# Flamingo layer with a mixture of experts on one core: keys of the first batch ahead, last V sum and last expert rows moved up, constant matmuls in the routing

## The chip, the cores and the metric

The kernel is written for Trainium2 and runs on one core. The metric is the device time of the kernel in microseconds (us), the median over runs. Five engines work side by side, each through its own list in order, and wait for each other through counters (semaphores): TensorE (PE, matmuls into PSUM), VectorE (DVE), ScalarE (ACT), GpSimd (POOL), SyncE (SP, which here only starts transfers). ACT, SP and POOL each start DMA transfers from their own queue.

## The reference, cut to what matters

Four batches of 512 tokens with 256 features (16 tiles of 128 tokens, "T"), a context of 1,601 rows per batch, and 8 experts of which each token uses 2.

```python
x = x + tanh(g_xattn) * xattn(layernorm(x), ctx, seg_id, Wq, Wkv, Wo)
x = x + tanh(g_ffn) * ffn(layernorm(x), gate_w, w1, b1, w2, b2)

def xattn(q, kv_src, seg_id, Wq, Wkv, Wo):      # 16 heads of 16
    qh = heads(q @ Wq.T); k, v = split(kv_src @ Wkv.T)
    # each token looks at 4 context rows: seg_id, seg_id-1, -2, -3
    scores = (qh . k_sel) * 16**-0.5; probs = softmax(masked scores over the 4)
    return (probs . v_sel) @ Wo.T

def ffn(x, gate_w, w1, b1, w2, b2):
    top_v, top_i = top_k(softmax(x @ gate_w.T), 2)
    # out = sum over the two experts e: top_v[e] * (silu(x @ w1[e] + b1[e]) @ w2[e] + b2[e])
```

## The kernel before

**Start.** SP loads the segment numbers, Wkv, Wq, Wo and x of batches 1 to 3 (L366 to L371), ACT the first 128 context rows of all batches (`ctx0`, one transfer), x of batch 0 and small things (L594 to L602). TensorE turns Wkv (L825) and the context (L831) by transposes. ScalarE and VectorE copy them out of PSUM; `keys_values(b)` (L857) makes keys and values of a batch, which go through `kv_sb` to a table `near_rows` in HBM, one per batch (L397). If no segment number is 128 or above, the rows beyond 128 aren't needed; that is the case here, and the branches under `general` are not taken. GpSimd's `gather(u)` (L514) fetches for the 128 tokens of tile u their 4 rows of keys and values (1 MB) by an indirect DMA; it runs 4 tiles ahead and has 8 slots. `first_norms` computes 1/sigma and the shift of the layer norm on GpSimd, first for batch 0, then after gather(0) for the other twelve tiles at once.

**Attention, 16 steps t.** VectorE's `step(t)`: product of the keys with the query (L1207), sum by head (L1211), mask, maximum, exponent on ScalarE (L644), sum, reciprocal, `prob` (L1232); within it `residual(t-2)` (L1241, L1244) and `second_moments(t-2)` (L1250). After step 0 VectorE also makes `gate2` (L1256) and `b2_lo` (L1258). GpSimd multiplies V by `prob` (`values`, L489; for the last tile it does half of the columns and VectorE the other half, L1264), makes the second norm (`norms`, L496 to L504) and the low half of each token (`remainder`, L526). TensorE: `query` (L874), `first_turn` (L882), `values` (L893: sums the 4 rows and turns them), `outputs` (L902, Wo), `second_turn` (L915), `logits` (L926). ScalarE: `first_x` (L631), `first_turned` (L638), `attended` (L652, copy of what `values` made), `second_x` (L661), `first_half` (L668), `token_out` (L673), `second_turned` (L679), `logits_kept` (L684). The order on each engine is written out by hand; after the loop comes a tail in which the last tiles are interleaved. SP loads the experts' weights (16 transfers of 1 MB, L362) during the steps and stores each x (L414).

**Routing.** VectorE runs a chain of small operations in which each waits for the one before through the counter `rt` (`link`): softmax and top 2 for tiles 0 to 11 while the last four tiles are still in work, then for these, cumulated counts, the list of tiles by expert, `order_i`, the tile count `tiles_i` (`RT_TILES`), the slots' rows `slot_row` (`RT_SLOT`), `tile_e` (`RT_LIST`). TensorE helps with short matmuls (L976 to L1006 and the list, L990), ScalarE with `pad_hot`, `e_col`, `e_pad` (L762 to L772).

**Experts.** Tiles of 128 slots, at least 32 (`FULL`) and here 37. Step q (`expert_steps`): TensorE makes the up product of tile q+1 (`up_chunk`, L1034, 48 matmuls of 128 columns) and the down product of tile q-1 (`down_chunk`, L1048 to L1056), interleaved while q+1 < FULL and one behind the other after that, and turns tile q+2 (L1062). ScalarE applies SiLU (L798) and splits weights (L780). VectorE copies the turned tile (L1449), splits weights (L1426), splits h in two 16-bit halves (`halves`, L1438 and L1440) and scales the finished rows (L1469, L1472). GpSimd gathers tokens (L576) and adds the rows to the output (L584), each addition only after the one before has landed.

## Time and profile before

| what | us |
|---|---|
| median of 3 runs (lowest, highest) | 364.44 (364.33, 365.71) |
| profiled execution | 364.77 |
| its span in the trace | 363.1 |
| busy: TensorE matmuls | 308.9 (85%) |
| busy: VectorE | 270.9 (75%) |
| busy: GpSimd | 204.8 (56%) |
| busy: ScalarE | 172.6 (48%) |

The busy shares are means over stages with different limits. In the stretch 45 to 60 us VectorE is busy for 14.24 of 15 us, in 150 to 200 us TensorE for 50.00 of 50, and between 110 and 130 TensorE for only 5.83 of 20. The profiled execution is 1.7 us longer than its span.

### The profile page before, as it was taken

The page shows a single profiled execution, that of the slowest core. Times are in us where ns is not written, and L with a number is a line of the kernel's source. Part 1 is how long each engine was busy: PE and PEld are TensorE (multiplying, and loading weights), DVE is VectorE, ACT ScalarE, POOL GpSimd, SP SyncE. Part 2 cuts the span into 40 slices and gives each one's busy share as a digit, 9 for nine tenths or more (in the row PEclk, how much of TensorE's full clock was granted, in tenths as well). Part 3 has the DMA queues.
Part 4 walks back from the last instruction along what each step waited for, and adds up shares of the span by engine and source line. Part 5 has one row for each costly group of instructions (what it writes and reads, how often), then busy time and mean ns, then how long its engine had stood idle before and what let it go on. Part 6 is the DMA issues. An engine that isn't in the chain of part 4 may idle for free.

```text
span 363.1 us, 10808 instructions
## 1 busy us (share of the span) xinstructions
PE 308.9 (85%) x3168; PEld 252.7 (70%) x3168; DVE 270.9 (75%) x641; ACT 172.6 (48%) x486; POOL 204.8 (56%) x226
## 2 busy tenths in 40 slices
PE   2767989999973349999999999999999999998910
PEld 2436878889862248788888888888888888786600
DVE  4848999999948976868878788787887776566510
ACT  1422256565454447655565565655656544324200
POOL 2286588886763052465737757477574675452330
PEclk9996999999995559999999999999999999999975
DMA  7689999999999421132323233233232332322121
GB/s 229 211 293 391 412 409 405 409 367 361 308 382 387 145 61 34 17 50 49 54 46 60 38 58 48 46 61 47 46 50 45 61 50 42 62 31 31 20 31 14
DMA packets 31388, 53.20 MB, mean 147 GB/s; under 512 B 4818, under 2 KB 25538, under 8 KB 29284
## 3 DMA queue, kind: packets, MB, share of 16 engines
q0 software_dynamic: 9408, 26.63, 28.8%
q1 hardware_dynamic: 16100, 22.57, 17.4%
q10 hardware_dynamic: 5824, 3.26, 3.0%
q8 instruction: 33, 0.54, 0.6%
q14 instruction: 23, 0.19, 0.2%
HBM read 42.29 MB, written 10.17 MB: 144 GB/s over the span
## 4 chain that ended last, share of the span: by engine, by line
PE 66%; POOL 10%; DVE 8%; issue 6%; DMA 6%; ACT 2%; POOLq 0%; SPq 0%; ACTq 0%; DVEq 0%
PE ps L1034 27%; PE ps L1048 15%; PE ps L1051 8%; PE ps L893 3%; DMA sel<-near_rows,win_near 3%; PE ps L1062 2%; PE ps L1056 2%; POOL w_parts L489 2%; POOL sel L489 2%; PE ps L902 2%; DMA w_parts<-in_L_xattn_Wkv 2%; POOL sel L514 1%; PE ps L1055 1%; PE ps L1050 1%; POOL rstd L499 1%
## 5 line engine op out<-in xcount | busy, mean ns | idle before, releaser
L1034 PE MATMUL ps<-sel,w_parts 128*128 128x128 f16 x1776 | 142.3, 221 | 0.6 <-DVE sel L1449 0.6
L1034 PEld LDWEIGHTS ps<-sel,w_parts 128*128 x1776 | 120.7, 99 | 25.0 <-issue 1.1
L798 ACT ACTIVATE sel<-ps,b1T 128x128 f32<-128x128 f32 x296 | 84.5, 369 | 92.4 <-PE ps L1034 86.8
L584 POOL DMA_INDIRECT out<-sel x37 | 62.7, 1694 | 88.7 <-DVE sel L1472 79.4
L1048 PE MATMUL ps<-w_parts,sel 128*128 x259 | 96.3, 379 | 2.1 <-DVE sel L1440 1.9
L1051 PE MATMUL ps<-w_parts,sel 128*128 x259 | 70.6, 273 | 0.0
L1440 DVE SCALAR_TENSOR_TENSOR sel<-sel 128x512 f16<-128x512 f32 x74 | 51.3, 693 | 2.5
L576 POOL DMA_INDIRECT sel<-tokens_split,sel x37 | 42.0, 1136 | 19.4 <-DVE sel L1408 12.7
L1426 DVE SCALAR_TENSOR_TENSOR w_parts<-w_parts (+1 forms) x32 | 39.0, 1220 | 8.6 <-issue 6.4
L571 POOL TENSOR_TENSOR sel<-sel 128x1 f32<-128x1 f32 x37 | 40.3, 1090 | 3.4 <-PE ps L1062 3.4
L1438 DVE TENSOR_SCALAR sel<-sel 128x512 f16<-128x512 f32 x74 | 33.1, 447 | 8.9 <-ACT sel L798 8.6
L780 ACT ACTIVATE w_parts<-w_parts (+1 forms) x32 | 34.1, 1067 | 7.9 <-issue 4.3
L1449 DVE COPY sel<-ps 128x512 f16<-128x512 f16 x37 | 15.7, 424 | 29.0 <-PE ps L1062 20.7
L1048 PEld LDWEIGHTS ps<-w_parts,sel 128*128 128x128 f16 x259 | 25.3, 98 | 7.6 <-issue 2.9
L1051 PEld LDWEIGHTS ps<-w_parts,sel 128*128 128x128 f16 x259 | 25.3, 98 | 3.7
L902 PE MATMUL ps<-WT,aT 128*128 128x256 f32 x64 | 18.4, 409 | 2.6 <-ACT aT L652 1.8
L874 PE MATMUL ps<-WT,xnT 128*128 128x256 f32 x64 | 17.1, 391 | 4.0 <-ACT xnT L638 4.0
L1469 DVE TENSOR_SCALAR xn<-ps,sel 128x256 f32<-128x256 f32 x37 | 17.7, 479 | 3.7 <-PE ps L1056 3.1
L893 PEld LDWEIGHTS ps<-ident,sel 128*128 128x128 f32 x128 | 16.9, 209 | 3.5 <-POOL sel L489 3.2
L489 POOL TENSOR_TENSOR sel<-sel,prob 128x1024 f32<-128x1024 f32 x8 | 15.6, 1952 | 6.3 <-DVE prob L1232 6.3
L893 PE MATMUL ps<-ident,sel 128*128 128x128 f32 x128 | 17.6, 296 | 1.7 <-POOL sel L489 1.7
L1062 PE MATMUL ps<-ident,sel 128*128 128x128 f16 x148 | 14.8, 224 | 4.9 <-DMA sel<-tokens_split,sel 4.9
(220 smaller groups left out, 441.4 us busy)
## 6 DMA issues: line engine op xcount, KB each, us to landing
w_parts<-in_L_ffn_w SPq DMA_DIRECT2D x16, 1024.0 KB
out<-xs SPq DMA_DIRECT2D x16, 128.0 KB
tokens_split<-xsplit ACTq DMA_DIRECT2D x16, 128.0 KB, 6.2
xs<-in_x SPq DMA_DIRECT2D x3, 512.0 KB, 11.0
near_rows<-w_parts SPq DMA_DIRECT2D x4, 256.0 KB, 2.9
sel<-tokens_split,sel POOLq DMA_INDIRECT x37, 2.9
out<-sel POOLq DMA_INDIRECT x37
w_parts<-in_ctx ACTq DMA_DIRECT2D x1, 512.0 KB, 4.3
```

What stands on the lines that cost most here:

```text
L571: pool.tensor_tensor(slot_w[:, at(q + 1)], xg[(k + 1) % 4][:, bass.ds(e + D, 1)], valid[:, at(q + 1)], ALU.mult).then_inc(s["slot_w_ok"], 1)
L576: pool.indirect_dma_start(xg[k], None, xd, bass.IndirectOffsetOnAxis(slot_row[:, at(q + 4)], 0))\
L584: pool.indirect_dma_start(out_rows, bass.IndirectOffsetOnAxis(slot_row[:, at(q - 1)], 0), y_sb[(k + 3) % 4], None, compute_op=ALU.add).the ...
L780: act.activation(part(to, 0), place(raw), ACT.Copy, scale=W_SCALE).then_inc(s["w_hi_ok"], 1)
L798: act.activation(h32[n][:, c * P:c * P + P], ps_h[n][:, c * P:c * P + P], ACT.Silu, bias=biases[:, c:c + 1], scale=1.0 / (X_SCALE * W_SCALE))\
L893: mm = pe.matmul(ps_a[:, c * P:c * P + P], slot(u)[:, j, D + c * P:D + c * P + P], ident[:, :], start=(j == 0), stop=(j == WIN - 1))
L1034: mm = pe.matmul(ps_h[n][:, c * P:c * P + P], w, xx, start=(i == 0), stop=(i == len(products) - 1))
L1048: pe.matmul(sides, hi, both, start=(c == 0), stop=False)
L1051: mm = pe.matmul(ps_y[n][:, 0:D], lo, rhi, start=False, stop=False)
L1426: v.scalar_tensor_tensor(out=part(to, 1), in0=place(raw), scalar=W_SCALE, in1=part(to, 0), op0=ALU.mult, op1=ALU.subtract).then_inc(s["w_l ...
L1438: v.tensor_scalar(h_hi[n][:, cols], h32[n][:, cols], H_SCALE, None, ALU.mult).then_inc(s["hhi_ok"], 1)
L1440: v.scalar_tensor_tensor(out=h_lo[n][:, cols], in0=h32[n][:, cols], scalar=H_SCALE, in1=h_hi[n][:, cols], op0=ALU.mult, op1=ALU.subtract). ...
```

## The change

It does seven things.
1. The context of batch 0 is loaded and turned by itself (`ctx_in0`, `context_turn`), ahead of Wkv; `keys_values(0)` follows directly. The other contexts come on SP's queue and are turned after query(0). x of batches 2 and 3 is loaded after the write of batch 0's keys.
2. Gather(1) goes ahead of the second `first_norms`; VectorE and ScalarE get the copies of the keys in another order.
3. `b2_lo` moves from VectorE to GpSimd, `gate2` behind the attention; the shift of the second norm is one operation per column on GpSimd instead of two in a chain.
4. In the tail of the attention, `values(T - 1)` comes before second_turn(T-4), its second column half first; `attended(T - 1)` and `logits_kept` change places on ScalarE.
5. TensorE gets 51 matmuls of 256 columns on constants, whose result nobody reads (`spin`).
6. `r_end` and `tiles_i` are computed after the slots.
7. For the tiles from FULL on, VectorE scales the finished rows (`rows_out`) before the first halves of the next tile.

```diff
 # SP
-            for b in range(1, B):
+            sp.dma_start(ctx0[:, 1:B, :], ctx_first[:, 1:B, :]).then_inc(s["ctx_in1"], 16)
+
+            def tokens_in(b):
                 sp.dma_start(xs[:, TPB * b:TPB * b + TPB, :], x_v[:, TPB * b:TPB * b + TPB, :]).then_inc(s[f"x_in{b}"], 16)
+            tokens_in(1)
...
             for b in range(B):
-                sp.wait_ge(s[f"kv_ok{b // 2}"], b % 2 + 1)
+                if b == 2:
+                    sp.wait_ge(s["kv_ok1"], 1)
+                else:
+                    sp.wait_ge(s["kv_ok0"], min(b, 2) + 1)
                 sp.dma_start(kv_near[b], kv_sb[:, b, :]).then_inc(s[f"kv_out{b}"], 16)
+                if b == 0:
+                    tokens_in(2)
+                    tokens_in(3)
 # GpSimd
-                pool.tensor_tensor(shift2[:, some], mv2[:, some, 0], rstd2[:, some], ALU.mult)\
-                    .then_inc(s["shift2_ok"], 1)
-                pool.wait_ge(s["shift2_ok"], 2 * i + 1)
-                pool.tensor_scalar(shift2[:, some], shift2[:, some], -1.0, None, ALU.mult)\
-                    .then_inc(s["shift2_ok"], 1)
+                for c in range(some.start, some.stop):
+                    last = pool.tensor_scalar(shift2[:, c:c + 1], mv2[:, c:c + 1, 0], rstd2[:, c:c + 1], -1.0, ALU.mult,
+                                              ALU.mult)
+                last.then_inc(s["shift2_ok"], 1)
...
-            gather(0)
+            for u in range(2):
+                gather(u)
             first_norms(2, slice(TPB, T))
-            for u in range(1, 4):
+            for u in range(2, 4):
                 gather(u)
+            pool.wait_ge(s["b2_hi_ok"], 1)
+            pool.tensor_scalar(b2_raw[:, :], b2_raw[:, :], 16.0, None, ALU.mult).then_inc(s["b2_lo_ok"], 1)
+            pool.wait_ge(s["b2_lo_ok"], 1)
+            pool.tensor_tensor(b2_lo[:, :], b2_raw[:, :], b2_hi[:, :], ALU.subtract).then_inc(s["b2_lo_ok"], 1)
 # ScalarE
-            act.dma_start(ctx0, ctx_first).then_inc(s["ctx_in"], 16)
+            act.dma_start(ctx0[:, 0, :], ctx_first[:, 0, :]).then_inc(s["ctx_in0"], 16)
...
             first_x(0)
+            act.wait_ge(s["wT_ps"], 1)
+            act.activation(WqT.rearrange("p k c -> p (k c)"), ps[:, 6, :], ACT.Copy).then_inc(s["wT_ok"], 1)
+            act.wait_ge(s["segt_ps"], 1)
+            first_turned(0)
             first_x(1)
-            first_turned(0)
+            act.activation(WoT.rearrange("p k c -> p (k c)"), ps[:, 7, :], ACT.Copy).then_inc(s["wT_ok"], 1)
             act.wait_ge(s["kv_ps"], 2)
             act.activation(kv_sb[:, 1, :], kv_bank[1], ACT.Copy).then_inc(s["kv_ok0"], 1)
             first_x(2)
             first_turned(1)
+            act.wait_ge(s["kv_ps"], 4)
+            act.activation(kv_sb[:, 3, :], kv_bank[3], ACT.Copy).then_inc(s["kv_ok0"], 1)
...
             first_half(T - 4)
+            token_out(T - 5)
+            attended(T - 1)
             logits_kept(T - 5)
             second_turned(T - 4)
-            token_out(T - 5)
-            logits_kept(T - 4)
             second_x(T - 3)
-            attended(T - 1)
             first_half(T - 3)
             token_out(T - 4)
             act.wait_ge(s["rt"], RT_SHIFT)
             act.activation(r_ex[:, 0:LATE, :], r_tmp[:, 0:LATE, :], ACT.Exp).then_inc(s["rt_exp"], 1)
+            logits_kept(T - 4)
             second_x(T - 2)
 # TensorE
+            pe.wait_ge(s["ctx_in0"], 16)
+            context_turn(0, 0, 0).then_inc(s["ctxT_ps"], 1)
             pe.wait_ge(s["wkv_in"], 16)
...
+            keys_values(0)
...
+            first_turn(0)
+            query(0)
+            pe.wait_ge(s["ctx_in1"], 16)
+            context_turn(1, 3, 0)
+            context_turn(2, 3, 256).then_inc(s["ctxT_ps"], 1)
+            context_turn(3, 2, 0).then_inc(s["ctxT_ps"], 1)
+            keys_values(1)
+            first_turn(1)
             pe.wait_ge(s["wT_ok"], 2)
-            pe.wait_ge(s["ctxT_ok1"], 1)
-            first_turn(0)
-            keys_values(1)
-            query(0)
-            first_turn(1)
             for b in range(2, B):
                 keys_values(b)
...
             outputs(T - 2)
+            values(T - 1)
             second_turn(T - 4)
             logits(T - 5)
-            values(T - 1)
+            outputs(T - 1)
             logits(T - 4)
-            outputs(T - 1)
             pe.matmul(ps_base, ones16[:, :], r_cum[:, :, :].rearrange("p e t -> p t e"), start=False, stop=True)\
                 .then_inc(s["rt_ps"], 1)
+
+            def spin(n):
+                for _ in range(n):
+                    pe.matmul(ps[:, 5, 0:2 * P], ones16[:, :], twice[:, :, :], start=True, stop=True)
+
+            spin(16)
             pe.wait_ge(s["rt"], RT_FIRST)
...
+            spin(4)
             pe.wait_ge(s["pad_hot_ok"], E + 1)
             for e in range(E):
                 mm = pe.matmul(ps_pad[0:E, 0:P], tok_e[:, e, :], pad_hot[:, e, :], start=(e == 0), stop=(e == E - 1))
             mm.then_inc(s["pad_ps"], 1)
+            spin(4)
             pe.wait_ge(s["rt"], RT_ROWS)
             rows_into_list(0, 8)
+            spin(2)
...
             rows_into_list(16, 24)
+            spin(1)
             pe.wait_ge(s["rt"], RT_ROWS + 3)
             rows_into_list(24, 2 * T).then_inc(s["list_ps"], 1)
+            spin(24)
 # VectorE
             first_norm(0)
-            for b in range(1, B):
-                first_norm(b)
-            for b in range(2, B):
-                dve.wait_ge(s["kv_ps"], b + 1)
-                v.tensor_copy(kv_sb[:, b, :], kv_bank[b]).then_inc(s["kv_ok1"], 1)
+            first_norm(1)
+            dve.wait_ge(s["ctxT_ps"], 2)
+            v.tensor_copy(ctxT[:, 1:3, :, :].rearrange("p b k c -> p (b k c)"), ps[:, 3, :]).then_inc(s["ctxT_ok1"], 1)
+            dve.wait_ge(s["ctxT_ps"], 3)
+            v.tensor_copy(ctxT[:, 3, :, :].rearrange("p k c -> p (k c)"), ps[:, 2, 0:256]).then_inc(s["ctxT_ok1"], 1)
+            first_norm(2)
+            first_norm(3)
+            dve.wait_ge(s["kv_ps"], 3)
+            v.tensor_copy(kv_sb[:, 2, :], kv_bank[2]).then_inc(s["kv_ok1"], 1)
...
-            link(v.tensor_tensor(r_end[:, :], r_first[:, :], r_tf[:, :], ALU.add))
-            link(v.tensor_reduce(tiles_i[:, :], r_end[:, :], AX_X, ALU.max))
-            assert done[0] == RT_TILES
...
             assert done[0] == RT_SLOT
+            link(v.tensor_tensor(r_end[:, :], r_first[:, :], r_tf[:, :], ALU.add))
+            link(v.tensor_reduce(tiles_i[:, :], r_end[:, :], AX_X, ALU.max))
...
+                if q + 1 >= FULL and live(-1):
+                    rows_out(q, k, m)
                 if live(1):
                     with filled(dve, tiles, q + 1):
                         halves(q + 1, m, 0)
-                if live(-1):
-                    with filled(dve, tiles, q - 1):
...
+                if q + 1 < FULL and live(-1):
+                    rows_out(q, k, m)
```

## Rows read from the trace of the kernel before

**Rows 1.** Chain that ended last, 0 to 34 us: start, us, what

```profile
10.82 2.35 PE ps L857 x4
...
13.81 2.87 DMA near_rows<-w_parts
...
17.61 1.23 POOL sel L514
...
22.70 0.48 POOL sel L514
...
24.10 9.39 DMA sel<-near_rows,win_near
...
33.58 1.23 DVE sel L1207
```

**Rows 2.** Timeline of VectorE: start, us, engine, line, operation, idle before

```profile
24.07 1.22 DVE L1207 TENSOR_TENSOR sel<-sel,ps 128x1024 f32<-128x1024 f32 x1 [0.91 <-DMA sel<-near_rows,win_near]
...
28.37 0.40 DVE L1258 SCALAR_TENSOR_TENSOR b_lo<-x,b_hi 8x256 f16<-8x256 f32 x1
...
29.01 1.22 DVE L1207 TENSOR_TENSOR sel<-sel,ps 128x1024 f32<-128x1024 f32 x1 [0.24 <-DMA sel<-near_rows,win_near]
...
95.57 1.19 DVE L1207 TENSOR_TENSOR w_parts<-w_parts,ps 128x1024 f32<-128x1024 f32 x1
```

**Rows 3.** Table by stretches: busy by engine (count), clock, DMA share, GB/s

```profile
13.00:14.00 1.00, 1.00 (x9) 0.78 (x7) 0.79 (x3) 0.60 (x1) 0.92 (x2) 1.00 1.06 346
...
17.00:18.00 1.00, 1.00 (x5) 0.50 (x4) 1.00 (x7) 0.04 (x1) 0.39 (x1) 1.00 0.00 0
```

**Rows 4.** Timeline, end of the attention

```profile
102.63 2.03 PE L893 MATMUL ps<-ident,w_parts 128*128 128x128 f32 x16
...
105.64 0.36 ACT L652 ACTIVATE aT<-ps 128x256 f32<-128x256 f32 x1
...
106.39 0.59 ACT L661 ACTIVATE x<-xs,shift,rstd 128x256 f32<-128x256 f32 x1
...
110.01 0.60 ACT L661 ACTIVATE x<-xs,shift,rstd 128x256 f32<-128x256 f32 x1
```

**Rows 5.** Table by stretches, a stretch after the attention

```profile
110.00:111.00 1.00, 0.34 (x2) 0.29 (x2) 0.96 (x15) 0.61 (x2) 0.00 (x0) 0.77 1.09 385
```

**Rows 6.** Timeline, end of the routing and first expert tiles

```profile
125.96 0.45 PE L990 MATMUL ps<-sel 128*128 128x39 f16 x8 [0.16 <-DVE sel L1375]
...
126.58 0.17 DVE L1392 TENSOR_TENSOR r_end<-r_first,r_tf 128x8 f32<-128x8 f32 x1
...
128.37 1.10 POOL L576 DMA_INDIRECT sel<-tokens_split,sel  x1 [12.74 <-DVE sel L1408]
129.36 2.36 DVE L1426 SCALAR_TENSOR_TENSOR w_parts<-w_parts 128x1024 f16<-128x1024 f16 x2 [1.16 <-ACT w_parts L780]
...
131.31 0.61 PE L1062 MATMUL ps<-ident,sel 128*128 128x128 f16 x4 [4.91 <-DMA sel<-tokens_split,sel]
...
132.52 2.10 PE L1034 MATMUL ps<-sel,w_parts 128*128 128x128 f16 x18 [0.60 <-DVE sel L1449]
...
138.17 1.18 PE L1034 MATMUL ps<-sel,w_parts 128*128 128x128 f16 x18
```

**Rows 7.** Timeline, last expert tiles

```profile
337.48 0.38 PE L1056 MATMUL ps<-w_parts,sel 128*128 x1
...
342.09 0.48 DVE L1472 SCALAR_TENSOR_TENSOR sel<-ps,sel,xn 128x256 f32<-128x256 f32 x1
...
343.34 1.72 POOL L584 DMA_INDIRECT out<-sel  x1 [5.25 <-DVE sel L1472]
...
344.14 0.48 DVE L1472 SCALAR_TENSOR_TENSOR sel<-ps,sel,xn 128x256 f32<-128x256 f32 x1
...
347.70 1.55 POOL L584 DMA_INDIRECT out<-sel  x1 [2.64 <-DVE sel L1472]
351.93 1.55 POOL L584 DMA_INDIRECT out<-sel  x1 [2.69 <-DMA out<-sel]
```

More of the change, by code:

```diff
@@ L567, in moe @@
                         pool.wait_ge(s["rt"], RT_LIST)
-                    with filled(pool, tiles, q + 1):
+                        tiles.append(tile_count(pool))
+                    with filled(pool, tiles[0] if tiles else None, q + 1):
                         e = pool.value_load(tile_e[0:1, at(q + 1)], min_val=0, max_val=E - 1)
@@ L573, in moe @@
                 if live(4):
-                    with filled(pool, tiles, q + 4):
+                    with filled(pool, tiles[0] if tiles else None, q + 4):
                         wait(pool, "slot_w_ok", q + 1)
@@ L580, in moe @@
                         pool.wait_ge(s["out_in"], 16 * T)
-                    with filled(pool, tiles, q - 1):
+                    with filled(pool, tiles[0] if tiles else None, q - 1):
                         wait(pool, "scattered", q * 16 - 16)
@@ L587, in _ @@
             expert_steps(moe, 4, 1)
-            wait(pool, "scattered", tiles * 16)
+            wait(pool, "scattered", tiles[0] * 16)
             pool.sem_inc(s["unused"], 1)
@@ L852, in _ @@
                 pe.wait_ge(s["g_kv"], B * (CHUNKS + 1))
-            def keys_values(b):
-                pe.wait_ge(s[f"ctxT_ok{b // 2}"], 1)
-                for c in range(KC):
-                    mm = pe.matmul(kv_bank[b], ctxT[:, b, c, :], WkvT[:, c, :], start=(c == 0), stop=(c == KC - 1))
-                mm.then_inc(s["kv_ps"], 1)
-            keys_values(0)
             pe.wait_ge(s["wraw_in"], 32)
@@ L943, in _ @@
             pe.wait_ge(s["small_T"], 2)
-            for n in range(2):
-                pe.wait_ge(s[f"kv_ok{n}"], 2)
+            pe.wait_ge(s["kv_ok0"], 3)
+            pe.wait_ge(s["kv_ok1"], 1)
             for t in range(1, T - 1):
```

82 lines of the change are left out of this document (41 added, 41 removed).

## Prediction

> **What bounds the kernel now.** I read the chain of waits first, then the timeline at the four places that the diff touches, then the busy table by stretches for clock and DMA.
>
> The start is one serial chain [rows 1]: keys and values of batch 0 on TensorE at 10.82, a copy, the write of `near_rows` at 13.81 (2.87 us to landing), the first gather at 17.61, data for VectorE at 24.07 [rows 2]. In it the DMA engines stand idle: the share between 17 and 18 us is 0.00 [rows 3]. The second gather is issued only at 22.70, because GpSimd computes the norms of twelve tiles between the two; the third gather, issued at 24.10, takes 9.39 us and ends at 33.49, and VectorE starts its step 2 at 33.58 [rows 1].
>
> From step 2 to step 15 VectorE alone sets the pace: L1207 runs at 33.58 and at 95.57 [rows 1, 2], 13 steps of 4.77 us, with no wait ahead of them. So what the start gains reaches the end of attention whole, and a faster GpSimd in the middle gains nothing.
>
> After that comes a latency chain through four engines: the last V sum on TensorE at 102.63, its copy on ScalarE at 105.64, the product and the residual behind it, the last normalised tile on ScalarE at 110.01 [rows 4]. In the routing VectorE is busy all the time and TensorE works little; its granted clock fell within the stretch 110 to 111 (mean 0.77) from 2.4 to 1.2 GHz [rows 5]. The expert stage begins at that lower level: 18 matmuls of 128 columns take 2.10 us at 132.52, and 1.18 us at 138.17, at full clock [rows 6]. From there on TensorE sets the pace to about 330. The end is a serial chain of scatters, each waiting until the one before has landed: issues at 343.34, 347.70, 351.93 [rows 7], about 4.3 us apart. What follows the last of them (11 us of span) is not touched.
>
> **Start: gain 2.1 us.** Batch 0 of the context comes alone, is turned before Wkv, and its copy (which ended at 10.3, right before the 10.82 of rows 1) leaves the chain. The chain then goes from the Wkv transposes (8.82) by their copies of 0.7 us to the keys at about 9.65: 1.2 us sooner, `near_rows` issued at 12.65. The sync queue now has 0.91 MB ahead of that write (Wkv, Wq, Wo, three contexts, x of batch 1) in place of 1.57 MB (three x loads, no contexts); the 0.66 MB less, at the 346 GB/s of the stretch 13 to 14 [rows 3], are 1.9 us. So it lands 1.2 to 1.9 us sooner; I take 1.5, at 15.2, and the first gather starts at 16.1, the second 1.5 us behind it.
>
> Two things push back. x of batches 2 and 3 (1 MB) now moves beside the first gather, though largely in the idle hole before its data; and TensorE turns the other three contexts only after query(0), near 17.7, so VectorE copies them until 18.3, does the norms of batches 2 and 3 until 21.8 and the keys of batch 2 until 22.6. Step 0 starts at 22.6 instead of 24.07: 1.5 us. The norm call on GpSimd then runs from 21.8 to 25.1 (18.9 to 22.2 before), gather(2) is issued near 25.4, 1.3 us later than now, but with no gather queued ahead of it. The gather that stood alone took 17.61 to 24.0, 6.4 us [rows 1, 2], so it lands near 31 to 32. Off VectorE go the two small operations after step 0: L1258 begins at 28.37 and step 1 at 29.01 [rows 2], some 0.5 us, and with gathers 1 and 2 in time the waits of 0.24 us ahead of steps 1 and 2. Steps 0 and 1 then take 8.7 us instead of 9.5. Step 2 starts at 31.3 instead of 33.58 by this sum; I take 2.1 us, with bounds of 0.5 (gather(2) as slow as today, 25.4 + 9.4, less what x no longer takes) and 2.8. On GpSimd the two b2 operations, some 1 us, and the late norms delay gather(4) and values(0) by about 2 us; values(t) has more than 4 us of slack to its reader two steps on, so this costs nothing.
>
> Weighed against a page: the Trainium skill, Trainium Kernel Development and Optimization, Key Constraints, says that the SP, ACT and POOL queues all share the same 16 DMA engines and interleave. The row with the idle engines [rows 3] says there is a hole for the moved loads to fill; were there none, by the rule the gather would share with 1 MB and the gain would sink to the 0.5 us above.
>
> **End of attention: gain 0.7 us.** values(15) is issued before second_turn(12) and logits(11): 0.6 us sooner, and its half for the columns that VectorE multiplies goes first. ScalarE then takes attended(15) before its other copies: at 104.1 instead of 105.64 [rows 4]. The residual gains about 1.3 us by it. But that is not what ends last: tile 15 at 110.01 stands on ScalarE behind logits 13 and 14, a chain of 3.6 us that starts with x(14) at 106.39 [rows 4], and starts near 105.8 after the change, since logits_kept(11) and exp now come ahead of x(14). The shorter shift (one operation on GpSimd instead of two, 0.3 us) is hidden by it. I put tile 15 at 109.3 to 109.4: 0.7 us, bounds 0 and 1.3 (all of the residual's gain).
>
> **Routing and the clock: gain 2.7 us.** Moving `r_end` and `tiles_i` behind the slots takes two links, 0.4 us, from 126.58 on [rows 6]: gather(0) starts 0.4 us before its 128.37, but the copy after the turn waits for VectorE's two weight splits, 129.36 to 131.7 [rows 6], so only 0.2 us of it arrives. The spins are matmuls of 256 columns. By the 18 matmuls of 128 columns at either clock (117 and 66 ns each [rows 6]) one costs 0.23 or 0.13 us: 27 of them before the list are 6.2 or 3.5 us, the 24 behind it 5.6 or 3.1. TensorE has idle time from 118.0 to 131.31 but for some 3 us of work, about 10 us. If the clock rises during the first 16 to 20 (4 us of unbroken work from 117.3; the expert stage needed 5.3 us of it, from 132.52 to 137.8) the list's matmuls end at 126.4 as now [rows 6] and the last 24 end near 129.5. Then turn(0) and up(0) run at full clock: up(0) starts at 132.3, and 48 matmuls and a turn at 66 ns are 3.3 us, so up(1) starts at 135.6 instead of 138.17 [rows 6], 2.6 us sooner. With the part above that is 2.7. The bounds: 3.0 above, and below a loss of 1.0 (clock low throughout: list 0.8 us late and the last spins still running at 131.3).
>
> **Tail: gain 2.3 us.** Tile 34's down product ends at 337.86, but its rows are scaled only after the halves of tile 36, until 342.57, and scattered at 343.34 [rows 7]. With rows_out ahead of these halves they are done at 338.9 and scattered at 339.7. That scatter has landed at 343.9, before tile 35 is ready (344.14 + 0.48), whose scatter then starts 0.77 us later at 345.4 instead of 347.70. Tile 36 follows 4.23 us behind at 349.6 instead of 351.93 [rows 7]: 2.3 us. Its own rows are ready at 347.7 or sooner, so this is not their limit. Cover gone, the least is 1.5 (scatters at 4.36 us and 0.4 us of more issue), the most 2.6.
>
> **Sum.** 2.1 + 0.7 + 2.7 + 2.3 = 7.8 us off the profiled execution's 364.77 (span 363.1 and 1.7 around it; the median of the runs is 364.44, 0.3 less): 357.0 us. Half a per cent, 1.8 us, is about what a measurement of this kernel can tell from no change.
>
> **Rivals.**
> - *The clock is low when up(0) begins* (chance 0.25). Between the last spin (129.5) and up(0) (132.3) there are only four transposes; in this trace the clock fell in the stretch 110 to 111 [rows 5], though TensorE was at work then with turns and matmuls of 8 columns. It costs 2.6 us and up to 0.8 more for the list: 359.6 to 360.4. The Trainium skill, TensorE: Matmul & The Clock Gate, Part 4, says that transposes do not count as busy for the clock; by it turn(0) holds nothing, and the fall beside the turns [rows 5] agrees.
> - *The start gives nothing* (0.15). gather(2) is 1.3 us later than now and VectorE waits at step 2 until 33.5. It decides from a landing 8 us after its issue. Against it: nothing is queued ahead of it. 359.1.
> - *Both of these*, 0.05: 361.5.
> - *Slower: the spins hold up the list and the turn* (0.03). If one spin costs not its columns but its whole latency, as the 0.38 us of the single matmul at 337.48 [rows 7], 51 of them are 19.4 us in a hole of 10: turn(0) is 9.4 us late, against the 7.8 us of gains: 366.4. It decides from 0.35 us each. Against it: 18 matmuls in 2.10 us are pipelined.
> - *One of the small parts fails* (tail or end of attention), 0.1: 357.7 to 359.3.
> - The forecast itself, 0.42: 355.7 to 358.2.
>
> **How the numbers follow.** 357.0 is the forecast case. From 354.6 (every part at its upper bound: 2.8 + 1.3 + 3.0 + 2.6 = 9.7, so 355.1, and 0.5 for the spread of runs) to 360.8 (the clock and part of the start lost) leaves out under 2 in 10. Faster by over 0.5% means below 362.6: all cases but the last spin case and mishaps of several parts, 0.93; within 0.5%, 0.04; slower, 0.03.
>
> **What would show it.** Step 2 of VectorE's L1207 at about 31.3 and 13 periods of 4.77 behind it; the third gather landing before it; the tile 15 normalised some 2.8 us before 110.01; the granted clock at 1.00 before 126 less the shift and still there when up(0) begins, with up(0) and its turn in 3.3 us; the last three scatters with the middle gap longer than the last one's 4.2. Wrong would be: VectorE waiting for DMA at step 2, a clock of 0.50 at up(0), list matmuls ending after VectorE is ready for them, or a new gap in the first expert tiles, where weight splits on VectorE (1.2 us each) could now be what up(1) waits for.

## The result, and the profile after

| kernel | median, us (lowest, highest, runs) | profiled execution | its span |
|---|---|---|---|
| before, on the same chip | 365.7 (364.33, 366.23, 9) | | |
| changed | 363.53 (362.39, 364.15, 9) | 364.15 | 362.3 |

The ratio is 0.9948 (95% interval 0.9933 to 0.9963): a gain of 0.5%, about 2 us, where 7.8 us were forecast. 363.53 lies outside the range of 354.6 to 360.8. Two of the four terms of the sum can be read off the trace at once: the tail came as forecast, and the start turned into a loss.

VectorE's steps (its product of keys and query, L1245 here, L1207 before), from the timeline of the changed kernel; the last row is the first operation of the late routing, which is at 113.17 in the kernel before:

```profile
23.28 1.22 DVE L1245 TENSOR_TENSOR sel<-sel,ps 128x1024 f32<-128x1024 f32 x1 [0.27 <-DMA sel<-near_rows,win_near]
...
27.52 1.21 DVE L1245 TENSOR_TENSOR sel<-sel,ps 128x1024 f32<-128x1024 f32 x1
...
35.51 1.22 DVE L1245 TENSOR_TENSOR sel<-sel,ps 128x1024 f32<-128x1024 f32 x1 [3.68 <-DMA sel<-near_rows,win_near]
...
40.92 1.19 DVE L1245 TENSOR_TENSOR sel<-sel,ps 128x1024 f32<-128x1024 f32 x1
...
98.46 1.19 DVE L1245 TENSOR_TENSOR w_parts<-w_parts,ps 128x1024 f32<-128x1024 f32 x1
...
115.85 0.19 DVE L1319 TENSOR_REDUCE r_mx<-logit 128x4 f32<-128x32 f32 x1 [1.32 <-ACT logit L693]
```

Step 2 is at 35.51 and not at 33.58 [rows 1], behind a wait of 3.68 us for its gather: 1.93 us late. Step 2 itself takes 5.41 us and not 4.77: 0.64 more. The last 0.33 us are lost between step 9 and step 10, which take 5.09 us. Such a step of 5.1 us stands at this place in all ten traces with the new start and in none of the four with the old one; the profile names no wait for it. So step 15 is at 98.46 and not at 95.57 [rows 2]. What stands before it, TensorE's and GpSimd's part of the same timeline (0 to 34 us):

```profile
9.53 3.75 PE L857 MATMUL ps<-w_parts 128*128 128x512 f32 x4 [0.83 <-ACT w_parts L621]
...
17.03 1.23 POOL L523 DMA_INDIRECT sel<-near_rows,win_near  x1 [3.91 <-DMA near_rows<-w_parts]
...
21.89 0.27 POOL L477 TENSOR_SCALAR rstd<-mv 128x12 f32<-128x12 f32 x1 [2.38 <-DVE mv L1225]
22.25 2.32 POOL L479 TENSOR_TENSOR rstd<-rstd,half 128x12 f32<-128x12 f32 x1
...
25.66 1.08 POOL L523 DMA_INDIRECT sel<-near_rows,win_near  x1 [0.45 <-issue]
...
29.84 1.02 POOL L523 DMA_INDIRECT w_parts<-near_rows,win_near  x1 [0.16 <-issue]
30.87 1.95 POOL L498 TENSOR_TENSOR sel<-sel,prob 128x1024 f32<-128x1024 f32 x1
```

Three things are to be seen. The keys of batch 0 start 1.3 us sooner than before, but take 3.75 us instead of 2.35 [rows 1]. Gather(2) is issued at 25.66, as forecast (25.4), but its data is there only at 35.5: 9.8 us, not the 6.4 assumed. And values(0), L498, whose input was ready at 27.6, starts at 30.87 behind the gathers and the b2 operations.

The end of the routing and the tail in the same timeline:

```profile
128.86 2.78 PE L1012 MATMUL ps<-twice,ones 128*128 128x256 f16 x24
...
130.97 1.08 POOL L590 DMA_INDIRECT sel<-tokens_split,sel  x1 [12.65 <-DVE sel L1441]
...
133.84 0.40 PE L1099 MATMUL ps<-ident,sel 128*128 128x128 f16 x4 [2.20 <-DMA sel<-tokens_split,sel]
134.88 2.10 PE L1071 MATMUL ps<-sel,w_parts 128*128 128x128 f16 x18 [0.64 <-DVE sel L1482]
...
341.43 1.56 POOL L598 DMA_INDIRECT out<-sel  x1 [3.63 <-DVE sel L1511]
347.04 1.54 POOL L598 DMA_INDIRECT out<-sel  x1 [4.05 <-DVE sel L1511]
351.17 1.54 POOL L598 DMA_INDIRECT out<-sel  x1 [2.59 <-DMA out<-sel]
```

Up(0)'s first 18 matmuls take 2.10 us, as before [rows 6]: the lower clock level again. The last three scatters stand at 5.61 and 4.13 us from each other, where they stood at 4.36 and 4.23 [rows 7].

The same two traces by the prediction's own terms (gains positive; up(1) begins at 138.17 before [rows 6] and at 139.49 after):

| part, from and to | before | after | gain | forecast |
|---|---|---|---|---|
| start: to step 15 | 95.57 | 98.46 | -2.89 | 2.1 |
| end of attention: to the late routing | 17.60 | 17.39 | 0.21 | 0.7 |
| routing and clock: to up(1) | 25.00 | 23.64 | 1.36 | 2.7 |
| experts and tail: to the last scatter | 213.76 | 211.68 | 2.08 | 2.3 |
| sum | 351.93 | 351.17 | 0.76 | 7.8 |

The two profiled executions differ by less than the medians (0.76 us against 2.17), and the loss at the start is larger in this trace than in others of the same start, as the next section shows.

### The profile page after: what moved, and what is told of

The parts are those of the page before. It is cut to its first block, busy times and chain, and to the rows that moved or that the text cites. A ratio compares the mean times of both kernels' runs of the same rounds, so it can differ in the third digit from the quotient of the medians.

```text
span 362.3 us, 10910 instructions
## 1 busy us (share of the span) xinstructions
PE 317.1 (88%) x3219; PEld 257.6 (71%) x3219; DVE 270.5 (75%) x640; ACT 172.9 (48%) x487; POOL 208.2 (57%) x224
## 3 DMA queue, kind: packets, MB, share of 16 engines
q10 hardware_dynamic: 5440, 2.87, 2.6%
## 4 chain that ended last, share of the span: by engine, by line
PE 64%; DVE 19%; issue 5%; POOL 4%; ACT 3%; DMA 1%; DVEq 0%; ACTq 0%; SPq 0%; POOLq 0%
PE ps L1071 28%; PE ps L1085 15%; PE ps L1088 8%; DVE ps L1249 4%; PE ps L1099 2%; PE ps L1093 2%; PE ps L916 2%; DVE w_parts L1245 2%; DVE sel L1245 2%; DMA w_parts<-in_L_xattn_Wkv 1%; DVE xs L1281 1%; PE ps L925 1%; PE ps L1087 1%; PE ps L1092 1%; PE ps L857 1%
## 5 line engine op out<-in xcount | busy, mean ns | idle before, releaser
L598 POOL DMA_INDIRECT out<-sel x37 | 64.1, 1732 | 84.5 <-DVE sel L1511 75.3
L590 POOL DMA_INDIRECT sel<-tokens_split,sel x37 | 44.7, 1209 | 19.2 <-DVE sel L1441 12.6
L585 POOL TENSOR_TENSOR sel<-sel 128x1 f32<-128x1 f32 x37 | 38.9, 1051 | 2.1 <-PE ps L1099 2.0
L1511 DVE SCALAR_TENSOR_TENSOR sel<-ps,sel,xn 128x256 f32<-128x256 f32 x37 | 17.9, 484 | 1.3
L498 POOL TENSOR_TENSOR sel<-sel,prob 128x1024 f32<-128x1024 f32 x8 | 15.5, 1936 | 5.7 <-DVE prob L1270 5.7
```

The source lines that it names most:

```text
L585: pool.tensor_tensor(slot_w[:, at(q + 1)], xg[(k + 1) % 4][:, bass.ds(e + D, 1)], valid[:, at(q + 1)], ALU.mult).then_inc(s["slot_w_ok"], 1)
L590: pool.indirect_dma_start(xg[k], None, xd, bass.IndirectOffsetOnAxis(slot_row[:, at(q + 4)], 0))\
L598: pool.indirect_dma_start(out_rows, bass.IndirectOffsetOnAxis(slot_row[:, at(q - 1)], 0), y_sb[(k + 3) % 4], None, compute_op=ALU.add).the ...
```

## The experiments

Twelve kernels in three groups of four, each group timed beside the kernel before, whose medians were 364.95, 364.98 and 365.1 us.

| run | median (lowest, highest) | ratio, 95% interval | step 15 | up(1) | last scatter |
|---|---|---|---|---|---|
| tail_only | 362.77 (361.7, 362.96) | 0.993, 0.9915 to 0.9946 | 95.45 | 138.06 | 349.43 |
| old_start | 361.9 (360.98, 364.64) | 0.9928, 0.99 to 0.9957 | 95.84 | 136.20 | 348.03 |
| no_spins | 363.52 (362.78, 364.22) | 0.9959, 0.9941 to 0.9977 | 97.57 | 138.90 | 350.58 |
| gathers_first | 362.94 (362.83, 364.78) | 0.9949, 0.9929 to 0.9968 | 98.27 | 138.52 | 350.51 |
| warm_start | 362.49 (361.74, 365.24) | 0.9945, 0.992 to 0.9971 | 96.62 | 136.56 | 349.00 |
| values_first | 358.59 (357.97, 359.74) | 0.9827, 0.98 to 0.9854 | 92.98 | 133.14 | 345.10 |
| gap_spins | 364.59 (362.68, 365.33) | 0.9981, 0.9963 to 0.9998 | 96.93 | 137.69 | 349.81 |
| old_gap | 363.03 (361.56, 364.88) | 0.9945, 0.9925 to 0.9966 | 95.45 | 136.24 | 348.70 |
| gap_few | 363.17 (361.79, 363.99) | 0.9938, 0.9914 to 0.9961 | 97.89 | 138.54 | 351.07 |
| gap_moved | 363.47 (361.52, 364.9) | 0.9951, 0.993 to 0.9972 | 96.85 | 137.10 | 349.28 |
| warm_vf | 359.66 (358.29, 362.56) | 0.9857, 0.9823 to 0.9892 | 94.09 | 134.05 | 346.58 |
| best | 359.49 (359.09, 360.31) | 0.9847, 0.9825 to 0.9869 | 92.96 | 134.18 | 346.71 |

Runs of one kernel spread by 1 to 4 us, so a median alone shows no difference of under 1 us. Each kernel has one trace, and traces spread too. Five of them have exactly the start of the changed kernel (its own, no_spins, gap_spins, gap_few, gap_moved): step 0 is at 21.97 to 23.28 in these and step 15 at 96.85 to 98.46. Four have the start of the kernel before (its own, tail_only, old_start, old_gap): step 15 is at 95.45 to 95.84. From step 0 to step 15 it is 74.60 to 75.34 us in the five and 71.50 us in the kernel before. The changed kernel's own trace is the latest of its five.

### tail_only: the tail's part alone

The kernel before, with only this of the change (cut; `rows_out` has the old lines unchanged):

```diff
+                if q + 1 >= FULL and live(-1):
+                    rows_out(q, k, m)
                 if live(1):
                     with filled(dve, tiles, q + 1):
                         halves(q + 1, m, 0)
-                if live(-1):
-                    with filled(dve, tiles, q - 1):
...
+                if q + 1 < FULL and live(-1):
+                    rows_out(q, k, m)
```

> The kernel before with rows_out alone moved up. Theory A (the scatter chain at the end is worth what the sum said): the last scatter is issued 4.9 us behind the end of tile 35's rows instead of 7.3, 2.3 us off the time, ratio 0.9937. Theory B (the tail gives nothing by itself, the first halves of the next tile are only delayed, and the gain seen between the traces is another part's): within 0.5 us of the kernel before, ratio 0.999.

Measured: 2.2 us under the kernel before. The last scatters in its timeline:

```profile
339.40 1.55 POOL L584 DMA_INDIRECT out<-sel  x1 [3.59 <-DVE sel L1478]
345.12 1.55 POOL L584 DMA_INDIRECT out<-sel  x1 [4.17 <-DVE sel L1478]
349.43 1.55 POOL L584 DMA_INDIRECT out<-sel  x1 [2.76 <-DMA out<-sel]
```

The last stands at 349.43 instead of 351.93 [rows 7]: 2.50 us, and it is again the one that waits for the scatter before it. Theory A. This one edit is worth as much as the whole change (2.18 us in the median against 2.17), so the rest together gives nothing that the medians show.

### old_start: the start of the kernel before

Against the changed kernel, cut to three places:

```diff
-            for u in range(2):
-                gather(u)
+            gather(0)
             first_norms(2, slice(TPB, T))
-            for u in range(2, 4):
+            for u in range(1, 4):
                 gather(u)
...
-            context_turn(0, 0, 0).then_inc(s["ctxT_ps"], 1)
...
-            keys_values(0)
```

> The changed kernel with the start of the kernel before (its loads, order of keys and gathers, b2_lo and gate2 on VectorE); all else as changed. Theory A (the new start costs 2.9 us, since the third gather arrives late and step 2 waits): step 2 of VectorE near 33.6 again, step 15 near 95.6, 2.9 us less than the changed kernel, ratio to the kernel before 0.987 to 0.989. Theory B (the start is neutral, the loss comes from the DMA load over the whole attention): step 15 stays near 98 and the ratio near 0.995.

Measured: 361.9, 1.6 us under the changed kernel; step 15 at 95.84 instead of 98.46. The start is a loss, as theory A says: by the nine traces above 1.0 to 3.0 us at step 15. In the time it is less than the 2.9 us of theory A, whose ratios of 0.987 to 0.989 lie below the measured interval of 0.99 to 0.9957. The wide spread of these runs leaves its size open.

### no_spins: without the 51 matmuls on constants

```diff
-            spin(16)
             pe.wait_ge(s["rt"], RT_FIRST)
...
-            spin(24)
```

> The changed kernel without its 51 constant matmuls. Theory A (the clock they raise falls again right before up(0), so they give only a faster turn, 0.2 us): ratio to the kernel before 0.995 to 0.996, up(0) at the low clock as in the changed kernel. Theory B (they are worth the 2.6 us of the prediction, or most of it): ratio 1.001 to 1.002.

Measured: 363.52, the changed kernel's time: theory A. From the late routing to up(1) it takes 24.06 us against 23.64, 0.42 more: 0.17 of it between turn(0) and up(0) (1.21 against 1.04 us, the turn is at the lower level), 0.25 in up(0).

### gathers_first: gathers 2 and 3 ahead of the norms

```diff
-            for u in range(2):
+            for u in range(4):
                 gather(u)
             first_norms(2, slice(TPB, T))
-            for u in range(2, 4):
-                gather(u)
```

> The changed kernel with gathers 2 and 3 issued before the norm call of the twelve tiles on GpSimd as well. Theory A (the third gather is late because it is issued at 25.7 us behind the norms): it is issued near 20, step 2 follows step 1 without a wait near 31.8, step 15 near 94.5, 3 us or more less than the changed kernel, ratio 0.986 to 0.988. Theory B (its arrival is set by the bytes on the DMA engines, not by its issue): step 2 stays near 35 and the ratio near 0.995.

Measured: 362.94. Step 2 now starts at 31.44 with no wait, 4.1 us sooner than in the changed kernel, as theory A says, and then lasts 9.3 us, which it doesn't say. The timeline on GpSimd, TensorE and VectorE:

```profile
30.35 1.08 POOL L523 DMA_INDIRECT w_parts<-near_rows,win_near  x1 [3.81 <-DMA near_rows<-w_parts]
31.46 1.95 POOL L498 TENSOR_TENSOR sel<-sel,prob 128x1024 f32<-128x1024 f32 x1
...
33.47 3.78 PE L914 MATMUL ps<-ident,sel 128*128 128x128 f32 x16 [5.11 <-POOL sel L498]
...
39.12 0.48 DVE L1279 SCALAR_TENSOR_TENSOR xs<-ps,tanh_g,xs 128x256 f32<-128x256 f32 x1 [4.41 <-PE ps L923]
```

Gather(4) waits 3.81 us for the second write of `near_rows`; behind it on GpSimd stands values(0), whose input has been ready since 27.3; behind that TensorE, idle for 5.11 us and then at the lower level (granted clock 0.50 from 28 us on; 3.78 us for 16 matmuls that take 1.95 later); behind that VectorE's residual. The low clock is nothing new here: in the kernel before the same 16 matmuls take 3.78 us too, at 30.62, but start 2.85 us sooner. The wait was exchanged for another.

### values_first: and gather(4) behind values(0)

```diff
-                if t + 4 < T:
+                if t == 1:
+                    gather(4)
+                if 1 <= t and t + 4 < T:
                     gather(t + 4)
```

> The kernel with all of the first four gathers ahead of first_norms on GpSimd, and now gather(4) behind values(0) instead of ahead of it. Theory A (in the run with the gathers first, step 2 to 3 took 9.3 us because values(0) stood behind gather(4), which waited 3.8 us for the second write of near_rows): values(0) starts at about 27.4, its matmuls at about 29.4, step 3 starts at 36 to 37 and not at 40.7, the last step at 94 to 94.5 and not at 98.3, and the time is 3 to 4 us under the changed kernel, about 359.5 to 360.5. Theory B (the half clock of TensorE's value matmuls, 3.78 us, was the reason): step 3 is gained only by 1 to 2 us, to about 39, time about 361.5. Theory C (the DMA engines are full in this stretch and the wait moves to gather(4) at step 4): steps 2 and 3 early, a wait of over 2 us for the gather ahead of step 4, and the same time.

Measured: 358.59, ratio 0.9827: theory A, 0.9 us under what it gave, and the lowest median of all versions. The timeline:

```profile
9.27 3.34 PE L857 MATMUL ps<-w_parts 128*128 128x512 f32 x4 [0.83 <-ACT w_parts L621]
...
26.61 1.93 POOL L498 TENSOR_TENSOR sel<-sel,prob 128x1024 f32<-128x1024 f32 x1 [0.21 <-DVE prob L1270]
30.04 1.08 POOL L523 DMA_INDIRECT w_parts<-near_rows,win_near  x1 [1.49 <-DMA near_rows<-w_parts]
...
30.68 1.21 DVE L1245 TENSOR_TENSOR sel<-sel,ps 128x1024 f32<-128x1024 f32 x1
...
35.46 1.19 DVE L1245 TENSOR_TENSOR sel<-sel,ps 128x1024 f32<-128x1024 f32 x1
...
92.98 1.19 DVE L1245 TENSOR_TENSOR w_parts<-w_parts,ps 128x1024 f32<-128x1024 f32 x1
```

From step 2 on the period is 4.77 but for the one of 5.1 us, and no step waits for data, though gather(4) still waits 1.49 us for its write. The 16 matmuls of values(0) still take 3.31 us, but start at 28.59, and step 3 is at 35.46: theory B, which blamed their clock and put it at about 39, is out. From step 0 to step 15 it is 70.77 us, 3.8 to 4.6 us less than in the five traces with the changed start. The new start, with this order on GpSimd, gains 2.59 us over the kernel before (95.57 to 92.98): the forecast's 2.1 was in it, but for the places of three gathers and one product in one queue.

### warm_start: TensorE kept busy at the start

```diff
+            pe.wait_ge(s["cast_consts"], 4)
+            spin(5)
             pe.wait_ge(s["seg_f"], 1)
...
             context_turn(0, 0, 0).then_inc(s["ctxT_ps"], 1)
+            spin(5)
             pe.wait_ge(s["wkv_in"], 16)
...
             mm.then_inc(s["wkvT_ps"], 1)
+            spin(6)
```

> The changed kernel with 16 more matmuls on constants on TensorE at the start: 5 before the segment turns, 5 between batch 0's context turns and the turns of Wkv, 6 between these and batch 0's key matmuls. Theory A (the start lost because the key matmuls of batch 0 ran at the low clock: 3.75 us against 2.35 before): the four matmuls of keys_values(0) take 1.9 to 2.4 us, the turns of Wq and Wo behind them stand 0.11 us apart and not 0.21, the first write of near_rows is issued at about 12.5 and not 13.95, gather(0) at about 15.6, and step 0 on VectorE starts about 1.3 us earlier, at about 22. Step 2 gains only a part of that, since the transfer of gather(2), issued behind first_norms, ends it. Time 0.3 to 1.3 us under the changed kernel. Theory B (the clock at the start does not follow from what TensorE does there): still 3.75 us and the same step times. Theory C (what the start decides is the transfer of gather(2) alone): the key matmuls are fast, step 0 is early, and step 3 starts at 40.9 as before, so no gain.

The timeline:

```profile
9.14 1.95 PE L865 MATMUL ps<-w_parts 128*128 128x512 f32 x4 [0.18 <-ACT w_parts L621]
...
14.84 1.22 POOL L523 DMA_INDIRECT sel<-near_rows,win_near  x1 [2.13 <-DMA near_rows<-w_parts]
...
25.19 1.08 POOL L523 DMA_INDIRECT sel<-near_rows,win_near  x1 [0.45 <-issue]
...
33.60 1.22 DVE L1249 TENSOR_TENSOR sel<-sel,ps 128x1024 f32<-128x1024 f32 x1 [2.49 <-DMA sel<-near_rows,win_near]
```

The keys take 1.95 us and gather(0) goes out at 14.84, 1.5 to 2.2 us sooner than in the five traces without these matmuls: theory A is right on the keys and the first gather. The steps gain nothing that can be told from the spread: step 0 is at 22.57 (21.97 to 23.28 without), behind VectorE's own norms and copies, step 2 waits 2.49 us for gather(2), and step 15 is at 96.62 (96.85 to 98.46 without). Which of the three places needed the matmuls was not tried.

### warm_vf and best: both together, and a filled gap

warm_vf is values_first with the matmuls of warm_start; best has those of gap_few (below) too.

> The version with all four first gathers ahead of first_norms and gather(4) behind values(0) (358.59 us), and the 16 matmuls on constants at the start. Theory A (the two causes of the lost start add): key matmuls of batch 0 in 1.9 to 2.4 us, gather(0) at about 15, step 0 at about 21 to 21.5, the last step at about 92, time 357.6 to 358.3. Theory B (step 0 is then held by something else, norms or the query of tile 0): step 0 at 22.2 as without the added matmuls and 358.6 again.

> The same, and the gap ahead of up(0) filled by the few long matmuls. Theory A: both gains add, 356.2 to 357.2 us. Theory B (the gap's matmuls give nothing): as the version without them, about 358.

Measured: 359.66 and 359.49, no better than values_first. Steps 0 and 15 stand at 23.28 and 94.09 in warm_vf, 22.19 and 92.96 in best, 22.21 and 92.98 in values_first: theory B. In all three VectorE does the norms of batches 2 and 3 and the copy of batch 2's keys before step 0, and waits for a gather 0.38 us at most.

### gap_spins, old_gap, gap_few and gap_moved: the gap ahead of up(0)

```diff
                 if q == -2:
                     registers_for(0)
+                    spin(16)
...
                             with filled(pe, tiles, q + 2):
                                 turn(q + 2)
+                if q == -2:
+                    spin(6)
```

This is gap_spins; old_gap is the same on old_start. Gap_moved adds these and drops the 24 spins of the first three places. Gap_few has, in place of the 22 (16 and 6), one matmul of 512 and one of 256 float32 columns (`ident` with rows of `xs`), and one of 256 behind turn(0).

> The changed kernel with 22 more matmuls on constants in the last part of the routing: 16 after the registers of tile 0 are loaded, while gather(0) of the experts is in flight, and 6 between turn(0) and up(0). Theory A (the clock fell during the 2.2 us idle time of TensorE ahead of turn(0), so that up(0) began at half clock): no fall of the granted clock between 131 and 139, the 48 matmuls of up(0) in 2.9 us and not about 4.3, up(1) some 1.2 to 1.5 us earlier, median 1.2 to 1.5 us under the changed kernel. Theory B (the clock falls there for another reason): the same 4.3 us. Theory C (the added matmuls hold up turn(0) or up(0)): turn(0) later by up to 0.5 us, which takes a third of the gain away.

> The changed kernel with the start of the kernel before (361.9 us in the earlier run, 361.0 to 364.6), and the same 22 matmuls on constants in the gap ahead of up(0). Theory A (its wide spread and a part of its time came from where the clock fell and rose around up(0)): up(0) at full clock in every execution, median 360.0 to 360.8 and the runs within 1.5 us of each other. Theory B (the spread came from the start or the transfers of the experts' weights): median 361 to 362 and a spread of over 2 us again.

> The changed kernel with the gap ahead of up(0) filled by few and long matmuls in place of 22 short ones: one of 512 and one of 256 columns in float32 on rows of x after the registers of tile 0, and one of 256 between turn(0) and up(0), each of which the chip runs as two passes, so 6 pairs of weight load and matmul. In the run with 22 the clock held but turn(0) began 4.1 us after gather(0) was issued and not 2.9. Theory A (it is the number of added instructions: a piece of the instruction stream was fetched in just that stretch, 16 KB on the transfer engines at about 130): turn(0) 2.9 us after gather(0), up(0) at full clock, up(1) about 1.2 us nearer to gather(0) than in the changed kernel, median 1.0 to 1.5 us under it. Theory B (matmuls that run while gather(0) is in flight delay turn(0) by themselves, whatever their number): again about 4 us, and no gain. Theory C (so little work doesn't hold the clock): turn(0) at 2.9 us and up(0) at half clock as in the changed kernel.

> The changed kernel with the 22 matmuls on constants in the gap ahead of up(0), and without the 24 in the first part of the routing, so that fewer matmuls stand ahead of turn(0) than in the changed kernel and the fetch of instructions falls behind it. Theory A (the fetch cost the 1.2 us): turn(0) 2.9 us after gather(0), up(0) at full clock, no fetch of the 16 KB kind in the 4 us ahead of turn(0), median 1 to 1.5 us under the changed kernel. Theory B (the matmuls themselves): 4.1 us again and the time of the changed kernel.

| run | gather(0) | turn(0) after it | up(0) to `r_prev` | gather(0) to first scatter |
|---|---|---|---|---|
| before | 128.37 | 2.94 | 5.53 | 21.39 |
| changed | 130.97 | 2.87 | 4.49 | 20.18 |
| gap_spins | 128.66 | 4.09 | 3.76 | 21.21 |
| old_gap | 127.18 | 4.11 | 3.78 | 21.25 |
| best | 125.36 | 3.89 | 3.81 | 21.00 |
| gap_few | 130.57 | 2.86 | 3.95 | 20.24 |
| gap_moved | 128.59 | 3.46 | 3.91 | 20.66 |
| warm_start | 128.58 | 2.88 | 3.95 | 20.27 |
| warm_vf | 126.08 | 2.91 | 3.78 | 20.20 |

(`r_prev` is a pair of small matmuls right behind up(0). The last two rows have the gap of the changed kernel.) The clock held in all five kernels with matmuls in the gap. It also held in two of the six that have the other spins and an unfilled gap, warm_start and warm_vf, so whether it is low at up(0) isn't set by the gap alone. None of the five is clearly faster than the kernel that it was made from; the spread of 3.3 us in old_gap is theory B's, and gap_few and gap_moved lie 0.4 and 0.1 us under the changed kernel, where their theories A gave 1.0 to 1.5. There are two reasons. First, in three of them turn(0) is over 1 us late. In these three one packet of 16 KB of the instruction stream (queue q8) moves between gather(0) and turn(0). The DMA queues of gap_spins from gather(0) to turn(0), 128.5 to 133 us (packets, MB, share):

```profile
q0 software_dynamic: 83, 0.27, 20.4%
q8 instruction: 1, 0.02, 1.3%
...
```

And of gap_few in the same part, 130.5 to 133.5 us:

```profile
q0 software_dynamic: 48, 0.14, 16.6%
q14 instruction: 1, 0.01, 1.1%
```

So a turn over 1 us late and a fetch at this place go together in all fourteen traces: in these three, and in none of the eleven others, where the fetch comes behind turn(0). Matmuls in the gap are not enough: gap_few has them too and starts its turn after 2.86 us. That speaks for theory A of gap_few and against B. In gap_moved the fetch comes behind the turn, as its theory A says; its 3.46 us are its own spins, which began at the lower clock and ended at 132. Few and long matmuls are no sure remedy, since best has just these and the fetch all the same. What the fetch delays is the gather. The chain of gap_spins has its transfer right ahead of the turn at 132.75:

```profile
128.66 4.05 DMA sel<-tokens_split,sel
```

The fetch moves from 1.68 to 2.61 us after the gather's issue. All but two of the gather's packets of 4 KB have ended by then; these two run one after the other from 2.59 on and end at 3.47. In gap_few the last one ends at 2.51. The same stands in old_gap and best.

Second, full clock at up(0) buys almost nothing against a clock that comes back soon. With full clock and a turn on time the first scatter comes 20.20 to 20.27 us after gather(0) (gap_few, warm_start, warm_vf). Where the clock is low at first and back 2.9 to 3.2 us after the start of up(0), it comes after 20.18 to 20.27 (changed, gathers_first, values_first, old_start). Only a later return costs: 20.51 in no_spins (back after 3.7 us), 21.39 and 21.40 in the kernel before and tail_only (after 5.3). Where the time goes then, the chain of gap_few (start, us, what) shows, and one row of its table by stretches (clock in the third column from the end):

```profile
134.47 1.65 PE ps L1071 x18
...
138.61 1.44 PE ps L1071 x18
```

```profile
136.00:137.50 1.50, 1.50 (x27) 1.43 (x24) 1.35 (x3) 0.43 (x2) 0.50 (x2) 1.00 0.39 124
```

The same of the changed kernel, its chain:

```profile
134.88 2.10 PE ps L1071 x18
...
139.56 1.11 PE ps L1071 x18
```

and its table, where the clock is coming back:

```profile
137.50:139.00 1.50, 1.50 (x26) 1.50 (x23) 1.50 (x2) 0.81 (x4) 0.94 (x2) 0.82 0.25 73
```

At a clock of 1.00 throughout, gap_few takes 80 to 92 ns per matmul in these rows; the changed kernel, once its clock is back, takes 62, and 12.0 to 12.2 us behind gather(0) both begin up(2) (143.00 and 142.72). In up(0) and up(1) something else than the clock sets the pace. The register operations that work out each weight's address are the candidate (65 of them beside 101 weight loads in the rows of this line of gap_few, 134 to 143 us); this was not tried.

## Why the prediction was wrong

**Start: the step that failed.** The text has gather(2) issued near 25.4, "so it lands near 31 to 32", and took 2.1 us; the trace has -2.89. The issue is right (25.66) and so is step 0 (22.6 forecast, 21.97 to 23.28 in the five traces of this start). Wrong are the landing and what stands behind it in GpSimd's queue:
- The landing of gather(2) was taken from gather(0), which ran alone (6.4 us), though the row of gather(2) itself said 9.39 [rows 1]. Measured are 9.8 us here and 8.6 to 10.3 from issue to step 2 in the five traces. The lower bound of 0.5 used this very number but never added it up: 25.4 + 9.4 is 34.8, already 1.2 us behind 33.58, a loss. The rival "decides from a landing 8 us after its issue" named the mechanism, and its price, no gain, was too mild. Shown by gathers_first: issued ahead of the norms, the data is there when step 2 wants it.
- "values(t) has more than 4 us of slack [...], so this costs nothing": values(0) came 3.3 us behind its input and TensorE stood idle for 4.43 us ahead of it. Its matmuls then took 3.78 us and those of outputs(0) 2.06, at the lower level (3.78 and 1.39 in the kernel before). VectorE's residual waited 0.52 us for them, and step 2 lasted 5.41 us. It lasted 5.4 to 6.0 us in four of the five traces of this start and 4.80 in no_spins, where the clock was back at 35.3 and not at 39.1: the late product and the clock cost this together. That the queue costs it is shown by gathers_first, where the residual waited 4.41 us, against values_first, where it waited for nothing.

A third item was priced wrong and cost nothing in the end. The keys of batch 0 were put at their old 2.35 us. In the old order TensorE goes from the Wkv turns straight on to eight context turns; in the new one it is idle for 0.83 us between the Wkv turns and the keys, and they ran at the lower level: 3.75 us, which took away the 1.3 us by which they started sooner. That the level hangs on what TensorE did before is shown by warm_start (1.95). But there gather(0) went out up to 2.2 us sooner and the steps did not start clearly sooner, so no run shows this as a part of the loss.

The Trainium skill, Trainium Kernel Development and Optimization, Key Constraints, says that the queues share the DMA engines, and this trace agrees: 9.8 us for a gather beside 1.8 MB of other transfers (three writes of `near_rows` of 256 KB issued from 21.01 on, and 1 MB of weights). The prediction looked for idle engines at 17 to 18 us, where gather(0) is; gather(2) flies from 26 to 35, where the DMA share is 0.93 to 1.07 in stretches of 2 us.

**Clock: the rival happened, its price was wrong.** The clock was at 0.54 in 134.5 to 136 when up(0) began (chance given 0.25). But the price of 2.6 us per missed clock is refuted: forcing full clock gave nothing at the first scatter, and the 5.3 us at the lower level in the kernel before cost 1.2. Of the 1.36 us gained here, 0.08 is ahead of gather(0), 0.07 and 0.17 are before and after the start of turn(0), and 1.04 is up(0), where the clock rose 3.2 us after the start instead of 5.3. No_spins has 0.79 of this 1.04 without any spin. The 0.4 us of `r_end` and `tiles_i` came to 0.08: `slot_row` ends 0.94 us behind `order_i` instead of 1.32, but gather(0) starts 0.80 us behind it instead of 0.50, and why is open. The forecast took the whole stretch up(0) to up(1) down to 3.3 us; the least in any run was 3.89.

**End of attention: right in mechanism.** The profiled run gained 0.21, but values_first, gathers_first and old_start take 16.61 to 16.62 us from step 15 to the late routing, against 17.60: 0.98, where 0.7 was said. What took it away is the clock again. The changed kernel's table by stretches:

```profile
111.00:112.00 1.00, 0.53 (x3) 0.45 (x3) 0.96 (x15) 0.38 (x1) 0.15 (x1) 0.50 1.10 381
112.00:113.00 1.00, 0.58 (x3) 0.48 (x3) 1.00 (x17) 0.39 (x2) 0.00 (x0) 0.50 1.10 364
```

and that of gathers_first:

```profile
111.00:112.00 1.00, 0.61 (x4) 0.52 (x4) 0.97 (x15) 0.30 (x3) 0.00 (x0) 1.00 1.09 375
112.00:113.00 1.00, 0.36 (x2) 0.20 (x2) 1.00 (x15) 0.58 (x2) 0.00 (x0) 1.00 1.09 367
```

It fell 12.3 us after step 15 in the one and 14.9 us after it in the other, on the same program there. All twelve traces with the new end agree: where the clock fell 14.7 to 15.1 us after step 15 (six traces) the late routing starts after 16.60 to 16.62 us; after 13.9 and 13.7 it is 16.88 and 16.84; after 12.8 (two traces) 17.27 and 17.28; after 12.3 and 12.1 it is 17.39 and 17.56. The place of the fall was not forced in any run, so the cause rests on this agreement.

**Tail: right.** Forecast 2.3, measured alone 2.5 in the trace and 2.2 in the median. Rows of tile 35 are done at 346.27 (345.79 + 0.48), and from there the last scatter starts 4.90 us later instead of 7.31 [rows 7].

**Spins as a danger** (the slower rival): refuted, 24 take 2.78 us at the higher level and 16 take 3.59 at the lower; the list and turn(0) did not wait for them.

## What to carry to other kernels

When an instruction moves in an in-order queue, walk the whole queue behind it: here the places of three gathers and one product on GpSimd decided 3.8 to 4.6 us between step 0 and step 15, and the same new start was 1.3 to 2.9 us slower or 2.6 us faster than the old one. Before a term of one trace is explained to a tenth, look at the same stretch in other traces: this start put step 15 anywhere within 1.6 us. Price a transfer by the row of its own kind in its own stretch, and add a bound up before calling it a gain. Before counting on a faster clock, look whether a stretch at full clock runs at the pace that the clock would allow.

## What the runs showed of the hardware

- A clock column of 1.00 at the very start is no proof. The first clock record is at 11.56 us in the kernel before and at 15.16 in the changed one, and the column reads 1.00 ahead of it too, while the same matmuls of 512 float32 columns take 1.04 to 1.19 us or 0.59. The durations tell the level.
- In the kernel before TensorE did only transposes from 6.86 on (16 turns of 128 columns) and then the keys, of whose four matmuls the first took 1.04 us and the other three 0.59; the same pattern stands in all four traces with the old start. In the changed kernel, where the turns ended 0.83 us ahead of the keys, all four took over 1.04. By the rule cited in the prediction (the Trainium skill, TensorE: Matmul & The Clock Gate, Part 4: transposes do not count as busy) the turns ahead of the keys would have done nothing for the clock. These traces speak against it for float32 turns, and no run tried it by itself.
- Added instructions have a price beyond their own time: in three kernels an instruction fetch of 16 KB fell between gather(0) and turn(0), held up the gather's last packets, and turn(0) came 1.0 to 1.2 us late; in the eleven other traces it did neither.
- A lower clock at the start of the expert stage cost nothing at the first scatter when it was back within 2.9 to 3.2 us, 0.3 us after 3.7 and 1.2 us after 5.3.
- The granted clock changed level at places that differ between kernels that are the same there: the fall after the attention lay 12.3, 14.7, 15.1 and 14.9 us behind step 15 (changed, values_first, old_start, gathers_first). Runs of one kernel spread by 1 to 4 us; that this is the clock is likely and not shown.
